# Splitting both turned chunks of k into fp16 parts and forming M from fp16 products alone

## What is computed

```python
qh = softmax_over_head_dim(Wq @ layernorm(x)) * SCALE      # per head, 64 rows
kh = softmax_over_tokens(Wk @ ctx)                         # 512 rows x 1024 tokens
vh = Wv @ ctx
context = einsum('bhdn,bhen->bhde', kh, vh)
out = Wo @ einsum('bhde,bhdn->bhen', context, qh) + bo
x = x + out / max(norm(out, axis=channels), 1e-12) * g * sqrt(128)
x = x + (layernorm(x) @ dequant(qweight) + bias)
```

## Time and profile before

| | |
|---|---|
| median of 3 runs | 633.75 us (632.51 to 635.59) |
| the profiled execution, its own time | 635.1 us |
| its span | 633.3 us |
| one iteration in the middle (from one `transpose_k(2)` to the next) | 36.3 us |
| busy share PE / DVE / ACT / POOL | 94% / 86% / 80% / 87% |

### The profile page before, as it was taken

One profiled execution on the slowest core, in us unless ns is written; L12 is line 12 of the kernel. 1 busy time (PEld: TensorE's weight loads), 2 busy tenths in 40 slices (PEclk: granted clock), 3 DMA queues, 4 the chain that ended last, 5 costly groups with the idle time before them and its releaser, 6 DMA issues.

```text
span 633.3 us, 10844 instructions
## 1 busy us (share of the span) xinstructions
PE 596.1 (94%) x3431; PEld 380.6 (60%) x3447; DVE 543.2 (86%) x904; ACT 507.1 (80%) x789; POOL 548.9 (87%) x473
## 2 busy tenths in 40 slices
PE   4686799999999999999999999999999999998897
PEld 3454375656657575665657566665756666574654
DVE  4897789898988999888988988898898989889754
ACT  4888789797879879787988979797897978788442
POOL 4268879999999999999999999999899999999630
PEclk9888799999999999999999999999999999999999
DMA  9416658868596876868887885868698595848551
GB/s 324 108 36 147 120 140 152 208 97 208 116 151 184 157 189 129 187 125 171 167 138 184 142 202 117 179 143 141 182 152 198 121 194 116 154 116 162 111 141 67
DMA packets 246969, 96.19 MB, mean 152 GB/s; under 512 B 236136, under 2 KB 237952, under 8 KB 246912
## 3 DMA queue, kind: packets, MB, share of 16 engines
q1 hardware_dynamic: 240576, 72.42, 59.3%
q10 hardware_dynamic: 6336, 23.07, 10.7%
HBM read 28.85 MB, written 8.39 MB: 59 GB/s over the span
## 4 chain that ended last, share of the span: by engine, by line
PE 74%; DVE 9%; ACT 5%; issue 4%; DMA 3%; POOL 3%; SPq 1%; ACTq 0%; POOLq 0%; DVEq 0%
PE ps_m L1619 14%; PE ps_m L1493 7%; PE ps_k L1411 4%; PE ps_o L1503 4%; PE ps_o L1411 4%; PE ps_o L1412 4%; PE ps_o L1413 4%; PE ps_k L1413 4%; PE ps_k L1412 4%; PE ps_q L1411 3%; PE ps_q L1413 3%; PE ps_q L1412 3%; PE ps_ta L1472 2%; PE ps_o L1527 2%; PE ps_tb L1472 2%
## 5 line engine op out<-in xcount | busy, mean ns | idle before, releaser
L514 POOL TENSOR_TENSOR q_tok_lo<-q_exp,q_tok_hi 128x1024 f16<-128x1024 f32 x64 | 135.8, 2132 | 8.1 <-ACT q_tok_hi L748 7.3
L737 ACT ACTIVATE q_exp<-q_exp,w_unit 128x512 f32<-128x512 f32 x128 | 92.9, 726 | 53.4 <-DVE q_exp L1070 53.3
L486 POOL TENSOR_TENSOR q_exp<-q_exp,q_rec 128x1024 f32<-128x1024 f32 x63 | 119.9, 1904 | 4.9
L1065 DVE TENSOR_REDUCE q_nmax<-ps_q 128x8 f32<-128x512 f32 x128 | 86.9, 679 | 28.5 <-PE ps_q L1413 28.2
L1619 PE MATMUL ps_m<-w_int,x_parts 128*128 128x512 f16 x432 | 100.0, 379 | 0.3 <-DMA x_parts<-spare 0.2
L1070 DVE TENSOR_TENSOR q_exp<-ps_q,q_nmax 128x512 f32<-128x512 f32 x128 | 88.5, 692 | 4.4
L522 POOL TENSOR_TENSOR k_lo<-k_exp,k_hi 128x1024 f16<-128x1024 f32 x32 | 82.2, 2569 | 9.2 <-ACT k_hi L678 9.2
L1056 DVE TENSOR_REDUCE k_nmax<-ps_k 128x1 f32<-128x1024 f32 x64 | 77.1, 1205 | 5.2 <-PE ps_k L1413 4.9
L1493 PE MATMUL ps_m<-k_t,c_t 128*128 128x256 f32 x256 | 77.0, 383 | 0.0
L1077 DVE TENSOR_REDUCE q_sum<-q_exp 128x16 f32<-128x1024 f32 x64 | 76.9, 1201 | 0.0
L748 ACT ACTIVATE q_tok_hi<-q_exp 128x1024 f16<-128x1024 f32 x64 | 67.5, 1054 | 7.8 <-POOL q_exp L486 5.4
(11 more groups left out here) (221 smaller groups left out, 1461.7 us busy)
## 6 DMA issues: line engine op xcount, KB each, us to landing
x_res<-in_x ACTq DMA_DIRECT2D x16, 512.0 KB, 3.6
out_x<-y SPq DMA_DIRECT2D x15, 512.0 KB, 2.9
x_in<-in_x ACTq DMA_DIRECT2D x14, 512.0 KB, 4.8
c_in<-in_ctx ACTq DMA_DIRECT2D x14, 512.0 KB, 6.0
x_in<-in_x SPq DMA_DIRECT2D x2, 512.0 KB, 5.6
c_in<-in_ctx SPq DMA_DIRECT2D x2, 512.0 KB, 7.0
q_hi<-q_tok_hi SPq DMA_TRANSPOSE x64, 3.3
q_lo<-q_tok_lo SPq DMA_TRANSPOSE x64, 3.3
```

Source lines behind the costliest of these rows:

```text
L486: nc.gpsimd.tensor_tensor(pair, pair, rec.unsqueeze(2).to_broadcast([P, 2 * HEADS, DH]), ALU.mult).then_inc(qs_done, 1)
L514: nc.gpsimd.tensor_tensor(q_tok_lo[p % 2][:], q_exp[:, 2 * p:2 * p + 2, :].rearrange("p t d -> p (t d)"), q_tok_hi[p % 2][:], ALU.subtract ...
L737: nc.scalar.activation(q_exp[:, j, :], q_exp[:, j, :], ACT.Exp, scale=w_unit[:]).then_inc(qexp_done, 1)
L1065: nc.vector.tensor_reduce(q_nmax[:, j, :], heads, op=ALU.max, axis=AX_X, negate=True).then_inc(qmax_done, 1)
```

## The change

Chunks 2 and 3 of exp(k) are also held as fp16 high and low parts, and M is formed by `three` fp16 products of 512 columns per token block. For that:

- `exp_k` makes the lifted bias for all four chunks (L660 runs four times in an iteration, not twice).
- `move_tk` writes fp16 `k_t_hi` and not fp32 `k_t`; a new DVE function `low_tk(k)` subtracts it from PSUM into `k_t_lo`. It runs four times in each of the 16 iterations: `low_tk(0)` and `(1)` behind `scale_y(0)`, `low_tk(2)` and `(3)` behind `shift_q(5)`.
- `scale_y(1)` moves from in front of `shift_q(5)` to behind `low_tk(3)`.
- PE's `transpose_k(2)`, `transpose_k(3)`, `transpose_c` and `mix_m` wait for `low_tk` as well as for `move_tk`.
- The fp32 copy `c_t` of the turned context and its two ACT copies in an iteration are gone, and so is `k_t`.

```diff
-                    if j < TURNED:
+                    if j < PARTED:                              # PARTED = 4, TURNED = 2
...
-                    nc.scalar.activation(k_t[:, t0:t0 + 4, fc * P:(fc + 1) * P],
+                    fc = fc + TURNED
+                    nc.scalar.activation(k_t_hi[:, t0:t0 + 4, fc * P:(fc + 1) * P],
...
                     nc.scalar.activation(c_t_hi[1 - s][:, 4 * h:4 * h + 4, :], turned, ACT.Identity,
-                                         scale=c_fit[:]).then_inc(cthi_done, 1)
-                    nc.scalar.activation(c_t[1 - s][:, 4 * h:4 * h + 4, :], turned, ACT.Identity,
                                          scale=c_fit[:]).then_inc(tc_moved, 1)
...
+                def low_tk(k):
+
+                    t0, fc = 4 * (k % 2), TURNED + k // 2
+                    dve.wait_ge(tk_moved, TK * a + k + 1)
+                    if k == 0 and begun(a):
+                        dve.wait_ge(m_ready, a)
+                    part = (slice(None), slice(t0, t0 + 4), slice(fc * P, (fc + 1) * P))
+                    nc.vector.tensor_tensor(k_t_lo[part], (ps_ta, ps_tb)[k % 2][:].rearrange("p (t c) -> p t c", t=4),
+                                            k_t_hi[part], ALU.subtract).then_inc(tklo_done, 1)
...                                                          # DVE's order, iteration 0
                     pick_nibbles(3)
+                    low_tk(0)
+                    low_tk(1)
                     shift_q(3)
                     set_up_gains()
                     shift_q(4)
+                    low_tk(2)
+                    low_tk(3)
                     set_up_top()
...                                                          # DVE's order, the other iterations
                     scale_y(0)
+                low_tk(0)
+                low_tk(1)
                 if do_n:
                     abs_c()
                 shift_q(4)
                 invert_k()
                 sum_q(a, 1)
+                shift_q(5)
+                low_tk(2)
+                low_tk(3)
                 if do_f and i != END:
                     scale_y(1)
-                shift_q(5)
...                                                          # PE: transpose_c, transpose_k, mix_m
                         pe.wait_ge(tk_moved, TK * n + h - 1)
+                        pe.wait_ge(tklo_done, TS * n + h - 1)
...
                         pe.wait_ge(tk_moved, TK * a + k - 1)
+                        pe.wait_ge(tklo_done, TS * a + k - 1)
...
                         pe.wait_ge(tk_moved, TK * (a + 1))
+                        pe.wait_ge(tklo_done, TS * (a + 1))
...
-                        three(ps_m[:, 0:TURNED * P], c_t_hi[s][:, t, :], c_t_lo[s][:, t, :], k_t_hi[:, t, :],
-                              k_t_lo[:, t, :], start=(t == 0), stop=False)
-                        last = nc.tensor.matmul(ps_m[:, TURNED * P:], c_t[s][:, t, :], k_t[:, t, :], start=False,
-                                                stop=(t == TC - 1))
+                        last = three(ps_m[:], c_t_hi[s][:, t, :], c_t_lo[s][:, t, :], k_t_hi[:, t, :], k_t_lo[:, t, :],
+                                     start=(t == 0), stop=(t == TC - 1))
```

More of the change, by code:

```diff
@@ L50 @@
 TURNED = 2
+PARTED = 4
 PAIRS = STEPS // 2
@@ L110, in build @@
         c_lo = sb("c_lo", [P, N], F32R)
-        c_t = [sb(f"c_t{s}", [P, TC, P]) for s in range(2)]
         c_t_hi = [sb(f"c_t_hi{s}", [P, TC, P], F16) for s in range(2)]
@@ L140, in build @@
         k_lift = sb("k_lift", [P, 1])
-        k_bias = sb("k_bias", [P, TURNED])
+        k_bias = sb("k_bias", [P, PARTED])
         k_hi = [sb(f"k_hi{j}", [P, N], F16) for j in range(TURNED)]
         k_lo = [sb(f"k_lo{j}", [P, N], F16) for j in range(TURNED)]
-        k_t_hi = sb("k_t_hi", [P, TC, TURNED * P], F16)
-        k_t_lo = sb("k_t_lo", [P, TC, TURNED * P], F16)
-        k_t = sb("k_t", [P, TC, HID - TURNED * P])
+        k_t_hi = sb("k_t_hi", [P, TC, PARTED * P], F16)
+        k_t_lo = sb("k_t_lo", [P, TC, PARTED * P], F16)
         q_tok_hi = [sb(f"q_tok_hi{r}", [P, 2 * HID], F16) for r in range(2)]
@@ L252, in build @@
         tk_moved = sem("tk_moved")
+        tklo_done = sem("tklo_done")
         tc_ready = sem("tc_ready")
@@ L263, in build @@
         cfit_steps = sem("cfit_steps")
-        cthi_done = sem("cthi_done")
         ctlo_done = sem("ctlo_done")
@@ L320, in build @@
         TK = 2 * (HC - TURNED)
+        TS = 2 * (PARTED - TURNED)
         def pipeline(iteration):
@@ L661, in exp_k @@
                                              bias=k_lift[:]).then_inc(kbias_done, 1)
-                        act.wait_ge(kbias_done, TURNED * b + j + 1)
+                        act.wait_ge(kbias_done, PARTED * b + j + 1)
                         bias = k_bias[:, j:j + 1]
@@ L1053, in max_k @@
                         dve.wait_ge(kexp_done, 4 * (b - 1) + j + 1)
-                    if begun(b) and j < TURNED:
-                        dve.wait_ge(kbias_done, TURNED * (b - 1) + j + 1)
+                    if begun(b) and j < PARTED:
+                        dve.wait_ge(kbias_done, PARTED * (b - 1) + j + 1)
                     nc.vector.tensor_reduce(k_nmax[:, j:j + 1], ps_k[:], op=ALU.max, axis=AX_X,
@@ L1591, in spread_last_rs @@
                     pe.wait_ge(tk_moved, TK * NB)
+                    pe.wait_ge(tklo_done, TS * NB)
                     nc.tensor.matmul(ps_ta[:, 0:P], rs_parts[:].rearrange("p g r -> p (g r)"), ident16[:],
```

## The result

The changed kernel takes 667.76 us (median of 6 runs, 666.58 to 672.36), the kernel before 633.9 us beside it. The ratio is 1.054 with a 95% interval of 1.051 to 1.057: 34 us slower. The forecast was 670.8 us. Its two stalls are there, the first close to its size, the second a quarter shorter. That the total came within 3 us is partly luck, though: the loop cost 8 us less than the sum said, and the ends 4 us more.

What follows compares the result with a forecast made beforehand. PE was taken to bound the kernel, its work being the 36.31 us period. Both stalls make it 38.95: 34.3 us over 13 periods, with the ends 37.0, added to 633.75 gives 670.8 us; 653 to 684 for 8 in 10.

Steps and rivals of the forecast that it cites:

- two stalls: PE idle twice an iteration: 1.59 us before transpose_k(2) for low_tk(0), about 1.7 us before mix_g for move_m.
- the ends: Iterations 0, 1 and 15, outside the 13 periods: losses of 1.6, 0.6 and 0.5 us.
- Part 1: PE's mix_m products: token blocks 0.66 us instead of 0.76, a gain of 0.8 us an iteration, 13 us over 128 blocks.
- the seam: Between two iterations, where ACT's move_m follows exp_k(n, 1) and mix_m; ACT is only 0.2 us ahead of PE.
- The rival that PE is the only bound (621 us): The wait before transpose_k(2) is hidden and the whole gain on mix_m arrives: 621 us; chance 0.03.
- Part 2: Before transpose_k(2), PE stands still through scale_y(0) and low_tk(0): a loss of 1.59 us in each iteration.
- Part 3: Chain from project_q(5) to move_m: DVE takes 14.54 us from shift_q(5) to max_k(n, 1); PE waits about 1.7 us.
- the rival of 649 us: Only the stall before transpose_k(2) counts, DVE keeps up at the seam: period 37.3 us, 649 us; chance 0.14 for 645 to 662.
- The rest of the loop: From move_m to the next transpose_k(2): 0.74 and 13.07 us as before, plus 0.2 us for k_bias; period 38.95 us.
- The rival of 692 us: PE's clock falls after its idle times once in every second iteration, costing 21 us; chance 0.11 for all above 679 us.

Runs made afterwards that it cites:

- e2: The changed kernel without the low_tk subtractions and all waits for them, low part of chunks 2 and 3 left zero; 636.39 us, ratio 1.003 to the kernel before.
- e5: The changed kernel with scale_y(1) put back ahead of shift_q(5); 660.03 us, ratio 1.039 to the kernel before.
- e3: The changed kernel with low_tk(0) and low_tk(1) moved ahead of scale_y(0); 654.42 us, ratio 1.033 to the kernel before.
- e6: The changed kernel with low_tk(0) and low_tk(1) ahead of scale_y(0), and scale_y(1) ahead of shift_q(5); 646.72 us, ratio 1.017 to the kernel before.
- e8: The kernel before with the lifted bias for chunks 2 and 3 of k too; 638.84 us, ratio 1.004 to the kernel before.
- e11: The kernel before with move_m ahead of exp_k(n, 1) on ACT; 650.03 us, ratio 1.026 to the kernel before.
- e1: The changed kernel with low_tk subtracting from a constant SBUF operand, without the transposes' wait for it; 697.67 us, ratio 1.103 to the kernel before.
- e7: e6 with project_q(4) issued ahead of transpose_k(2) on PE; 643.53 us, ratio 1.011 to the kernel before.
- e9: e7 with move_m ahead of exp_k(n, 1) on ACT; 647.21 us, ratio 1.023 to the kernel before.
- e10: e9 with, in iteration 0, shift_q(3) ahead of low_tk(0), pick_nibbles(3) behind low_tk(1), and project_q(4) ahead of transpose_k(2); 647.86 us, ratio 1.024 to the kernel before.
- e12: e7 with the same edits to iteration 0 as e10; 644.57 us, ratio 1.013 to the kernel before.
- e4: The changed kernel with sum_q(a, 2) on DVE moved from in front of max_k(n, 0) to behind max_k(n, 1); 683.42 us, ratio 1.080 to the kernel before.

## Why the prediction was right, and where it was not

- **Part 1, the products of PE.** The blocks are 0.66 us apart, as forecast. PE's busy time fell by 8.0 us, not by about 13. The 13 periods before, and then in the changed kernel (PE's busy us and count, granted clock, DMA share, GB/s):

```profile
107.05:580.23 473.18, 470.30 (x2744) 1.00 0.75 158
```

```profile
113.97:613.47 499.50, 460.48 (x2536) 1.00 0.70 149
```

There it fell by 9.8 us, 0.76 a period, as forecast. Ahead of them it rose from 80.83 to 83.57 us, with a granted clock of 0.87 where it had been 0.92. That the gain would buy nothing at the seam held too: e2 has the gain without the subtractions and gets 0.23 us a period out of it. The rival that PE is the only bound (621 us) would have been wrong even without a single `low_tk`.
- **Part 2, the stall at `transpose_k(2)`.** Read from start to start in e5, where no record is missing, PE stands still for 377.90 - 376.04 - 0.22 = 1.64 us, against 1.59. `scale_y(0)` held DVE for 267.01 - 266.40 = 0.61 us and not 0.65, and the hand-over from the end of `low_tk(0)` to PE took 267.83 - 267.01 - 0.68 = 0.14 and not 0.05. e3 shows the cause, the place behind `scale_y(0)`: of the 1.64 us the order alone was 1.03.
- **Part 3, the chain to `move_m`.** Three terms of it were mis-sized. The chain from `shift_q(5)` to `max_k(n, 1)` took 14.08 us, not 14.54. An added instruction costs 0.60 us on DVE and not 0.65: the 0.65 was read between a `y` and a reduction, while two subtractions of this kind start 0.59 to 0.60 apart. That is 0.15 for three. The waits that go gave back more than their idle times: 0.38 and 0.51 are marked in the earlier trace rows, but from `mv` (261.10 by the same timeline of before) to `q_nmax` it was 0.60 and is now 278.46 - 278.34 = 0.12, and the second such place went from 0.71 to 0.13. An instruction that needn't wait also starts under the end of the one before it. Together these are 1.06 where 0.89 was put, and the instructions right behind the two places start 0.15 earlier as well. ACT's exponential took the 2.77 us of the sum (290.56 + 0.19 - 287.98), but `m_t` starts 0.10 us under its end. So PE waited 1.30 us at `mix_g` and not 1.7. That this second stall is a term of its own, which the rival of 649 us denied, is what e5 and e6 show.
- **The rest of the loop.** `k_bias` was given 0.2 us; e8 has 0.11. From `mix_g` to the end of `feed_forward(0)` the trace has 306.23 - 1.64 - 291.38 = 13.21 us, against 13.27 in the sum. The period is 38.40 for 38.95, and the 13 periods between the first `transpose_k(2)` in steady work and the last cost 26.3 us for 34.3.
- **The ends.** They were sized too small. PE before, in iteration 0:

```profile
32.14 0.63 PE L1472 MATMUL ps_ta<-ident,k_exp 128*128 128x128 f32 x4 [1.04 <-ACT k_t L757]
```

PE in the changed kernel:

```profile
35.44 1.09 PE L1491 MATMUL ps_ta<-ident,k_exp 128*128 128x128 f32 x4 [2.92 <-DVE k_t_lo L1120]
...
40.24 0.61 PE L1428 MATMUL ps_q<-wq_hi,xn_lo 128*128 128x512 f16 x1 [1.30 <-DVE q_exp L1069]
...
76.49 1.09 PE L1491 MATMUL ps_ta<-ident,k_exp 128*128 128x128 f32 x4 [2.55 <-DVE k_t_lo L1120]
...
113.97 0.63 PE L1491 MATMUL ps_ta<-ident,k_exp 128*128 128x128 f32 x4 [1.76 <-DVE k_t_lo L1120]
...
613.47 0.63 PE L1491 MATMUL ps_ta<-ident,k_exp 128*128 128x128 f32 x4 [1.69 <-DVE k_t_lo L1120]
```

The `transpose_k(2)` of iteration 2 starts at 113.97 instead of 107.05 us. Without its own stall of 1.76 that is 5.2 us late, where 1.6 + 0.6 = 2.2 were given. From there to the last one at 613.47 it is 499.50 us against 473.18, the 26.3 of the loop, and what is left behind it, with one stall, adds 1.2 for the 0.5 of the sum. 5.2 + 26.3 + 1.2 = 32.7 us, the difference of the two spans. The failing step is the one that counted the new instructions of iteration 0 at 0.65 us each: at the first such place PE comes to wait 2.92 us where it waited 1.04 us before. The granted clock of the first stretches may have its share. Before, then the changed kernel, then e8 and e11, from 35 to 55 us:

```profile
35.00:55.00 20.00, 15.77 (x90) 10.86 (x90) 17.10 (x37) 17.37 (x23) 14.84 (x15) 0.91 0.42 94
```

```profile
35.00:55.00 20.00, 15.76 (x62) 7.80 (x64) 17.71 (x35) 15.16 (x20) 13.07 (x13) 0.76 0.22 39
```

```profile
35.00:55.00 20.00, 14.44 (x89) 9.44 (x88) 16.59 (x36) 17.28 (x24) 14.62 (x14) 0.93 0.36 82
```

```profile
35.00:55.00 20.00, 13.75 (x80) 8.93 (x77) 18.46 (x36) 17.16 (x24) 12.98 (x13) 1.00 0.20 37
```

The third number from the end is the granted clock: it averages 0.76 in the changed kernel and 0.91 before, between the two levels of 1.2 and 2.4 GHz. (The counts of PE's instructions don't compare, since its new products are fewer and longer.) In the profiled executions of the kernels with `low_tk` (the changed kernel, e1, e3 to e7, e9, e10, e12) this stretch has 0.74 to 0.83; in the four without (before, e2, e8, e11) 0.91 to 1.00. How the late start splits between the waits and the clock stays open. The second `m_t` starts between 95.1 and 102.1 us among the kernels with low parts from PSUM, but in e11, which has none, it starts at 97.62, although the clock was 1.00 in this stretch (0.76 from 20 to 35 us, where before it was 0.89). And e6 and e7 have the same code in iteration 0, yet their first `m_t` starts at 52.3 and at 56.5 us, with 0.89 and 0.77 from 20 to 35 us.
- **The clock in the loop.** The rival of 692 us is out. Idle times of 1.6 and 1.3 us alternate in each period, and the granted clock is 1.00 in the window of all 13 periods shown above. By the page "TensorE: Matmul & The Clock Gate" of the Trainium skill, section on the clock gate (Part 1), the throttled state is the default and activity releases it; idle times of these two lengths did not bring it back, in any period of the loop.

## What to carry to other kernels

Where a new instruction reads a PSUM bank that PE is about to write again, its price is set by what stands in front of it in its engine's list, and not by its length alone: moving two instructions ahead of one other won 13 us here (e3). A gain on the busiest engine is worth only the slack of the next chain that leads to the same place (0.20 us of the 0.8 here), so test it alone, without the costs that come with it, as in e2. And size the first iterations by their own rows: a fifth to a quarter of this loss was outside the loop.

## What the runs showed of the hardware

DVE's subtractions of two operands in SBUF did not run beside POOL's tensor operations here; one waited for the other. `low_x2` is such a subtraction, of 1024 columns. In the changed kernel it starts under the end of POOL's `q_exp`; the row of DVE, and then those of POOL:

```profile
296.14 1.58 DVE L1207 TENSOR_TENSOR spare<-og,spare 128x1024 f16<-128x1024 f32 x1
```

```profile
294.74 1.90 POOL L486 TENSOR_TENSOR q_exp<-q_exp,q_rec 128x1024 f32<-128x1024 f32 x1
296.60 3.13 POOL L522 TENSOR_TENSOR k_lo<-k_exp,k_hi 128x1024 f16<-128x1024 f32 x1
```

POOL's `q_exp` ends at 294.74 + 1.90 = 296.64, DVE's subtraction at 296.14 + 1.58 = 297.72, 1.08 us later. In e4 it is 303.40 and 304.48, again 1.08, although the recorded duration is 3.12 us there. So the duration is that of a wait plus the same 1.08 us of work. Without a wait it is 1.21 us, as in e11, where POOL's operation ends at 287.50 + 1.90 = 289.40:

```profile
289.35 1.21 DVE L1197 TENSOR_TENSOR spare<-og,spare 128x1024 f16<-128x1024 f32 x1
```

The other way round, POOL's `k_lo`, which started while DVE was in its subtraction, is recorded with 3.13 us, where the same operation in e4, in front of DVE, has 2.14. The `low_tk` of the change reads one operand from PSUM and took 0.68 us every time (mean 681 ns, 64 times), beside whatever POOL did. With both operands in SBUF, in e1, its duration (least, median and longest of 64, in ns) was:

```profile
L1122 DVE TENSOR_TENSOR k_t_lo<-scale_bc,k_t_hi x64: 677/1243/2846, 39.2 to 651.7; 128x512 f16<-128x512 f32 x64
```

At the least it is as fast as with one operand in PSUM, so the place of the operand costs nothing by itself; what it costs is the wait. The pair of 3.98 us stood beside three of POOL's operations.

The Trainium skill, page "SBUF — State Buffer", section Who interferes with whom, states this: a DVE instruction with two SBUF inputs contends with a GpSimd instruction that reads SBUF, and the order of issue decides which of the two is blocked. The traces agree; the 1.08 us and the 1.0 us that POOL loses are this case's. What it means for orders written by hand is in e4: 1.4 us of DVE work moved behind the seam shortened the seam's wait by 0.6 us, and the kernel took 16 us more. `low_x2` started 0.10 us behind the start of a POOL operation of 2.1 us, where in the changed kernel the operation before it had only 0.5 us left to run.
